# A fused wavelet, attention and expert-choice kernel: the second half of the token selection moved among the first expert chunks, rows split by columns, GpSimd's subtractions in pieces

## The chip, the core and the metric

One core of a Trainium2 chip runs one program. The metric is device time in microseconds (us), the median of 3 runs. Engines: TensorE (PE, matmuls; its weight loads are PEld), VectorE (DVE), ScalarE (ACT), GpSimd (POOL) and SyncE (SP, which only issues DMAs here). "Row L1535" means line 1535 of the kernel before.

## The reference, cut to what matters

```python
h = wavelet(x, ...)                                   # [32, 256, 256]
h = concat([cls_tok, h], axis=1)                      # [32, 257, 256]: 8224 rows
h = h + attention(layernorm(h), R)
h = h + moe(layernorm(h), ...)

def moe(x, gate_w, gamma, beta, fc1s, b1s, fc2s, b2s):
    scores = (tanh(x @ gate_w.T) + 1) * 0.5           # [8224, 8]
    vals, idx = top_k(scores.T, 1028)                 # each expert takes its 1028 best rows
    y = layernorm(x[idx], gamma, beta)
    h = gelu(y @ fc1[e].T + b1[e])                    # 256 -> 1024
    o = (h @ fc2[e].T + b2[e]) * vals                 # 1024 -> 256
    return x.at[idx].add(o)
```

## The kernel before

**Ahead of the change.** Wavelet and attention run image by image until some 295 us. The unfinished sum goes to `out`, normalised rows with their gates go to `rows` in HBM. `V` holds the gates as [128, 2, 257]: partition = expert within a half (4) x image (32), middle axis = the half `eh` (experts 0 to 3, experts 4 to 7). Twelve rounds of counting find each expert's threshold `Tf`.

**Selection (L1487 to L1526).** VectorE marks gates above and equal to the threshold (`ge`, `eq`), with their counts. TensorE sums the counts over an expert's images with the 0/1 matrices `same` and `before`. VectorE ranks the equal ones by a scan, keeps as many as are needed, adds them to `ge` and scans again. `TB` then holds, for each half, the exclusive rank of each token within its image, the image's number and the image's first slot in bf16, high and low part. `begM` and `finM` hold the first and last slot of an image, masked to one expert in each column. All of it is done for both halves at once, and then comes the first expert. `link` is a wait of VectorE for its own last instruction.

**Placing.** `one_hot` writes `oh` [128, 1028]: slot s belongs to image p. It takes two instructions, `ohu` (L1535) and `oh` (L1538). `place` treats one tile of 128 of the 1028 slots (eight tiles and one of 4): TensorE multiplies `oh` with `TB` into a PSUM bank (L1001), VectorE copies three columns out (`SM`, L1553), takes `rk` (L1556), counts the ranks not above it (`jk`, `pos`, L1560), computes the row's base (`rowf`, L1562) and adds them to the index (`idx`, L1566). Each tile of TensorE waits (`smc`) until VectorE has read the one before.

**Experts.** A `Job` is an expert (`q` = 0 to 7 in order of time) and a chunk `c` of it: 3 tiles (384 rows), 3 tiles (384), 3 tiles (260), `j` = 3q + c. An expert's weights sit in one of two buffer sets, by `eh`. Experts go in the order 0, 4, 1, 5, ... (`e = el + 4 * eh`), so each buffer set belongs to one half of `V`. All float matmuls are three products of high and low parts in fp32r. In `emit` every engine has the same frame: eight slices `f` for the current job, with work of the previous and next one laced in. TensorE: the first layer of slice f (`first`, six matmuls of 384 columns, L1022), a share of the previous job's second layer (`second`, L1036 for tokens, L1048 for the tail chunk), at f = 3 the turn (transposes, L1011) of the next job's rows, tiles to place, at f = 6 `tail_back` (L1059). ScalarE: `hidden` (gelu L756, copy `hh` L759), at f = 1 and 3 of jobs with c = 0 and c = 2 the copy `high` (L722) of one half of the next weights into fp32r, at f = 4 `high_rows` (L729), and `weighed` (L772). VectorE: `low_hidden` (the remainder `hl`, L1590), `with_bias`, `tail_bias` (L1612), `scaled` (gamma and beta on the turned rows, L1575) at f = 3, `low_rows` (L1583) at f = 5, and `place`. GpSimd, in its own order: scatters (L577), gathers (L555), and `low` (L536), which subtracts the copied high part from `raw`. `first` of slice f waits for `low_hidden` of slice f - 3.

**Weights.** `raw` [128, 2048] is one buffer in two halves. SyncE loads a half (L436) when GpSimd's `low` of that half is done (`wlo0`, `wlo1`), in the order w1, w2 of each expert. w2 of the next expert is split in the jobs with c = 2, w1 of the one after it in those with c = 0.

**Tiles to place.** The tiles of an expert are placed ahead of it, spread over the slices of a job by `spread`; when the last is placed, the next expert's one-hot follows. In the first expert's jobs, expert 1's nine tiles and expert 2's nine are placed in jobs 0, 1 and 2 (7, 5 and 6 of them), job 3 has none; from job 4 on there are 4 and 5 in the jobs with c = 1 and c = 2.

```python
both = [(3, t) for t in range(9)] + [(6, t) for t in range(9)]
tiles = both[(0, 7, 12)[k]:(7, 12, 18)[k]]
...
if split and u:
    low(1 - cur.eh, cur.q + 1, cur.c // 2, u - 1)
```

## Time and profile before

| | us |
|---|---|
| median of 3 runs | 784.48 (784.38 to 785.78) |
| the profiled execution | 786.62 |
| its span, first to last instruction | 784.8 |
| busy: TensorE / VectorE / ScalarE / GpSimd | 696.7 / 541.0 / 459.9 / 473.3 |
| mean granted TensorE clock | 0.944 |
| scatter L577, mean of 72 | 1.58 |
| GpSimd's L499, mean of 37 | 0.24 |
| GpSimd's subtraction L536 of w2, mean of 16 | 2.41 |

A row of a timeline gives the start and the length in us, the engine, the line, the operation, what it writes and reads with partitions x elements, and in brackets how long the engine had stood before it and what released it. "x6" are six instructions merged into one row. Instructions of an engine overlap a little: the next may start before the last one's record ends.

### The profile page before, as it was taken

Reading aid. Unit: us, or ns where it says so; the run is one execution under the profiler, and the core shown is the slowest. Engines: PE = TensorE matmul, PEld = TensorE weight load, DVE = VectorE, ACT = ScalarE, POOL = GpSimd, SP = SyncE. Lnnn points to the kernel's source line nnn. Section 1 sums busy time; section 2 is a strip of 40 time slices with the busy share of each in tenths; the row PEclk is TensorE's granted clock in tenths of the full one; section 3 lists DMA queues with packets and bytes.
Section 4 is the critical chain, followed back from the end, with each engine's and each line's share of the span. In section 5 each row is a group of like instructions: output and inputs, shape, how many; then the busy total and the mean of one; then the engine's idle time right before and its main releaser. Section 6 shows DMA issues by size and latency. Waiting matters only on the chain.

```text
span 784.8 us, 15827 instructions
## 1 busy us (share of the span) xinstructions
PE 696.7 (89%) x4630; PEld 635.5 (81%) x4630; DVE 541.0 (69%) x1885; ACT 459.9 (59%) x1095; POOL 473.3 (60%) x660
## 2 busy tenths in 40 slices
PE   6987999999999945447999999989999999999994
PEld 3986888888888734336989999989889999899993
DVE  3765798998899778987784766756846757634431
ACT  1003588888888869315556656665566566656551
POOL 0258689888988545142366485584674855846523
PEclk9989999999999975559999999999999999999997
DMA  9900022222222228121134243352342432533222
GB/s 258 307 18 1 4 83 81 80 80 81 80 80 81 81 93 170 54 56 61 30 81 117 42 109 89 50 149 43 75 122 41 108 88 42 146 52 49 35 28 27
DMA packets 63563, 64.14 MB, mean 82 GB/s; under 512 B 14032, under 2 KB 57104, under 8 KB 63376
## 3 DMA queue, kind: packets, MB, share of 16 engines
q1 hardware_dynamic: 50576, 46.33, 19.6%
q0 software_dynamic: 12800, 17.12, 13.5%
q8 instruction: 26, 0.43, 0.2%
q14 instruction: 33, 0.27, 0.1%
q10 hardware_dynamic: 128, 0.00, 0.0%
HBM read 37.90 MB, written 25.53 MB: 81 GB/s over the span
## 4 chain that ended last, share of the span: by engine, by line
PE 36%; DVE 7%; issue 6%; ACT 6%; POOL 5%; DMA 3%; POOLq 0%; ACTq 0%; DVEq 0%; SPq 0%
PE bank L1022 16%; PE bank L1036 15%; ACT bank L746 2%; PE bank L1011 2%; PE bank L1048 2%; POOL out L577 2%; POOL w2l L536 1%; POOL yg L555 1%; DMA raw<-in_fc1T 1%; DMA yg<-rows,idx 1%; DVE yl L1583 1%; ACT bank L756 1%; PE bank L1001 1%; DVE jk L1560 1%; ACT hh L759 1%
## 5 line engine op out<-in xcount | busy, mean ns | idle before, releaser
L577 POOL DMA_INDIRECT out<-ob,sidx x72 | 113.9, 1582 | 160.5 <-ACT ob L772 148.8
L1590 DVE TENSOR_TENSOR hl<-bank,hh 128x384 fp32r<-128x384 f32 (+1 forms) x192 | 97.5, 513 | 139.1 <-ACT hh L759 138.6
L756 ACT ACTIVATE bank<-bank,b1s 128x384 f32<-128x384 f32 (+1 forms) x192 | 99.4, 518 | 138.0 <-PE bank L1022 133.5
L1022 PE MATMUL bank<-yh,w1h 128*128 128x384 f32 (+1 forms) x384 | 132.7, 346 | 8.1 <-DVE hl L1590 4.7
L1022 PE MATMUL bank<-yh,w1l 128*128 128x384 f32 (+1 forms) x384 | 123.8, 322 | 0.0
L1022 PE MATMUL bank<-yl,w1h 128*128 128x384 f32 (+1 forms) x384 | 123.3, 321 | 0.0
L1036 PE MATMUL bank<-w2h,hh 128*128 128x256 f32 x384 | 108.1, 281 | 0.0
L1036 PE MATMUL bank<-w2l,hh 128*128 128x256 f32 x384 | 108.0, 281 | 0.0
L1036 PE MATMUL bank<-w2h,hl 128*128 128x256 f32 x384 | 107.9, 281 | 0.0
L555 POOL DMA_INDIRECT yg<-rows,idx x72 | 72.4, 1006 | 44.2 <-issue 39.1
L759 ACT ACTIVATE hh<-bank 128x384 fp32r<-128x384 f32 (+1 forms) x192 | 87.7, 457 | 6.1
L1022 PEld LDWEIGHTS bank<-yh,w1h 128*128 128x128 f32 x384 | 73.8, 192 | 13.0 <-DVE hl L1590 6.0
L1022 PEld LDWEIGHTS bank<-yl,w1h 128*128 128x128 f32 x384 | 73.6, 192 | 0.0
L1022 PEld LDWEIGHTS bank<-yh,w1l 128*128 128x128 f32 x384 | 73.1, 190 | 0.0
L1036 PEld LDWEIGHTS bank<-w2h,hh 128*128 128x128 f32 x384 | 72.7, 189 | 0.0
L1036 PEld LDWEIGHTS bank<-w2l,hh 128*128 128x128 f32 x384 | 72.7, 189 | 0.0
L1036 PEld LDWEIGHTS bank<-w2h,hl 128*128 128x128 f32 x384 | 72.5, 189 | 0.0
L880 PE MATMUL bank<-ET,Rw 128*128 128x256 f32 x256 | 66.1, 380 | 1.7 <-ACT ET L663 1.7
L948 PE MATMUL bank<-GT,ET 128*128 128x137 f32 (+1 forms) x256 | 52.5, 340 | 0.7 <-ACT GT L690 0.7
L504 POOL TENSOR_TENSOR ST<-A,mhalf 128x6 f32<-128x6 f32 x37 | 50.0, 1352 | 3.1
L880 PEld LDWEIGHTS bank<-ET,Rw 128*128 128x128 f32 x256 | 43.8, 191 | 5.6 <-issue 2.1
L290 POOL TENSOR_TENSOR ARENA<-OB,C 128x512 f32<-128x512 f32 x32 | 40.8, 1275 | 12.2 <-ACT OB L637 12.2
(249 smaller groups left out, 1770.6 us busy)
## 6 DMA issues: line engine op xcount, KB each, us to landing
BIG<-in_x SPq DMA_DIRECT2D x4, 2048.0 KB, 16.3
out<-Bs SPq DMA_DIRECT2D x32, 256.0 KB, 2.2
rows<-Yp SPq DMA_DIRECT2D x32, 256.0 KB, 2.4
raw<-in_fc1T SPq DMA_DIRECT2D x16, 512.0 KB
raw<-in_fc2T SPq DMA_DIRECT2D x16, 512.0 KB
yg<-rows,idx POOLq DMA_INDIRECT x72, 2.8
out<-ob,sidx POOLq DMA_INDIRECT x72, 3.8
gwb<-in_gate_w SPq DMA_DIRECT2D x1, 1024.0 KB, 7.2
```

What stands on the lines that cost most here:

```text
L290: return ops.tensor_tensor(OP[m.p].rearrange("p g (r k) -> p g r k", k=CG), blocks.unsqueeze(2).to_broadcast(wide), cst("blocks").rearrang ...
L504: g.tensor_tensor(st[:, 8:14], A6[:, :], mhalf[:, :], ALU.pow).then_inc(s["pow"], 1)
L555: g.indirect_dma_start(out=yg[eh][0:m, t, :], out_offset=None, in_=rows, in_offset=tok(ap=idx[eh][0:m, t:t + 1], axis=0))\
L577: g.indirect_dma_start(out=out_rows, out_offset=tok(ap=sidx[job.eh][0:m, t:t + 1], axis=0), in_=ob[t % 3][0:m, :], in_offset=None, compute ...
L746: last = A.activation(sgn[2 * eh + j], V[:, eh, :], ACT.Sign, bias=tried[:, k:k + 1], scale=-1.0, accum_out=cna[eh][:, j:j + 1])
L756: A.activation(h[:, 0:cur.w], h[:, 0:cur.w], ACT.Gelu_apprx_tanh, bias=b1s[:, bass.ds(cur.e, 1), f]).then_inc(s["hact"], 1)
L759: A.activation(hT[cur.p][0][:, f, 0:cur.w], h[:, 0:cur.w], ACT.Copy).then_inc(s["hhi"], 1)
L880: last = T.matmul(Rb[:, e * D:(e + 1) * D], Rw[:, j, e * P:(e + 1) * P], ET[c.p][:, j, 1:NT], start=(j == 0), stop=(j == 1))
L948: T.matmul(Sb[:, c0:c0 + w], ET[c.p][:, j, 1 + h * P:1 + (h + 1) * P], GT[c.p][:, j, 0:w], start=(j == 0), stop=False)
L1022: last = T.matmul(Lb[ring(cur, f)][:, 0:cur.w], w1s[cur.eh][i][:, d, f * P:(f + 1) * P], yT[cur.p][k][:, d, 0:cur.w], start=(n == 0), stop ...
L1036: mm = T.matmul(bank[4 + t % 2][:, 0:D], hT[prev.p][i][:, f, at:at + P], w2s[prev.eh][k][:, f, :], start=(n == 0), stop=(n == 23))
L1590: v.tensor_tensor(hT[cur.p][1][:, f, 0:cur.w], Lb[ring(cur, f)][:, 0:cur.w], hT[cur.p][0][:, f, 0:cur.w], ALU.subtract).then_inc(s["hlo"], 1)
```

## The change

- **Experts in order.** `e = q`; an expert's half of `V`, `TB`, `begM` is `q // 4`, its column `q % 4`. Buffers still alternate with `q`.
- **Selection by halves.** The chain is cut into `above`, `ranked_at`, `asked_for`, `taken`, `ranked`, `slots`, `slots_of_images`. For half 0 they run in one go, as before. For half 1 they are laced into VectorE's jobs 2 to 5; TensorE's three small matmuls for it go to jobs 3 and 5 (`asked`, `begun`), into columns of bank 7 between two tiles, with waits `tk_read` and `tc` on the next tile. The image's first slot is read from PSUM without a link.
- **Placing.** `SM` is gone: `rk` and `rowf` read the PSUM bank directly, and `rowf` comes ahead of `jk`. In the first expert's six jobs the tiles are 4, 5, 4, 5, 4, 5.
- **Rows split by columns.** `turn`, `scaled`, `high_rows`, `low_rows` signal for each of the two halves of the 256 columns; `first` of slice 0 waits for each half ahead of its three matmuls. In the first expert `low_rows` stands behind tile 5 instead of tile 6.
- **GpSimd's `low`** is four instructions of 256 columns instead of one of 1024; only the last signals.
- **Tail's bias ahead.** `tail_bias` stands ahead of `low_hidden` of its slice instead of behind.
- `keep_index` of expert 1 waits for its nine indices.

```diff
+PIECE = 256
-                self.e = self.el + 4 * self.eh
+                self.e = self.q
+                self.half, self.group = (self.q // 4, self.q % 4) if isinstance(self.q, int) else (1, self.q - 4)
...
-                if isinstance(el, int) and el == 0 and k < 3:
-                    both = [(3, t) for t in range(9)] + [(6, t) for t in range(9)]
-                    tiles = both[(0, 7, 12)[k]:(7, 12, 18)[k]]
+                if isinstance(el, int) and el == 0:
+                    tiles = [(3 + k // 2 * 3, t) for t in ((0, 1, 2, 3), (4, 5, 6, 7, 8))[k % 2]]
...
-                rest = g.tensor_tensor(flat(lo, half), raw[:, half * NF:(half + 1) * NF], flat(hi, half), ALU.subtract)
+                for c0 in range(0, NF, PIECE):
+                    rest = g.tensor_tensor(flat(lo, half)[:, c0:c0 + PIECE], raw[:, half * NF + c0:half * NF + c0 + PIECE],
+                                           flat(hi, half)[:, c0:c0 + PIECE], ALU.subtract)
                 rest.then_inc(s[f"wlo{half}"], 1)
...
+                elif job.q == 1:
+                    po.wait_ge(s["ixd"], 2 * 9)
...
-                act.wait_ge(s["yr"], job.j + 1)
                 after(act, "hmm", (job.j - 1) * 8)
                 for d in range(2):
-                    last = A.activation(yT[job.p][0][:, d, 0:job.w], bank[2 + d][:, 0:job.w], ACT.Copy)
-                last.then_inc(s["yhi"], 1)
+                    act.wait_ge(s["yr"], job.j * 2 + d + 1)
+                    A.activation(yT[job.p][0][:, d, 0:job.w], bank[2 + d][:, 0:job.w], ACT.Copy).then_inc(s["yhi"], 1)
...
+            def asked(half, total):
+                pe.wait_ge(s["tk_c"], 2 * half + 1)
+                T.matmul(total[:, 0:1], cst("same"), cgt[:, half:half + 1], start=True, stop=True)
+                T.matmul(total[:, 1:2], cst("before"), tot[:, half:half + 1], start=True, stop=True).then_inc(s["tk_mm"], 1)
+            def begun(half, total):
+                pe.wait_ge(s["tk_c"], 2 * half + 2)
+                T.matmul(total[:, 2:3], cst("before"), tot[:, half:half + 1], start=True, stop=True).then_inc(s["tk_mm"], 1)
+            asked(0, bank[2])
+            begun(0, bank[2])
...
+                if t == 4 and isinstance(job.q, int) and job.q == 2:
+                    pe.wait_ge(s["tk_read"], 2)
+                if t == 4 and isinstance(job.q, int) and job.q == 3:
+                    pe.wait_ge(s["tc"], 2)
...
+                    if f == 0 and n % 3 == 0:
+                        pe.wait_ge(s["yt"], cur.j * 2 + d + 1)
...
-                    pe.wait_ge(s["yt"], cur.j + 1)
...
+                    if at_job(cur, 3) and f == 0:
+                        pe.wait_ge(s["smc"], 2 * 9 + 4)
+                        asked(1, bank[7])
+                    if at_job(cur, 5) and f == 0:
+                        pe.wait_ge(s["smc"], 3 * 9 + 4)
+                        begun(1, bank[7])
...
+            def slots_of_images(half, total):
+                h, n = slice(half, half + 1), slice(NT + 1, NT + 2)
+                dve.wait_ge(s["tk_c"], 2 * half + 2)
+                dve.wait_ge(s["tk_mm"], 2 * half + 2)
+                v.tensor_tensor(fin[:, h], total[:, 2:3], tot[:, h], ALU.add)
+                v.tensor_copy(beg[:, h], total[:, 2:3])
+                link(v.tensor_copy(TB[:, half, n], total[:, 2:3]))
+                link(v.tensor_copy(mm2[:, h], TB[:, half, n]))
+                v.tensor_tensor(TB[:, half, NT + 2:NT + 3], beg[:, h], mm2[:, h], ALU.subtract)
+                for e in range(2):
+                    last = v.tensor_tensor((begM, finM)[e][:, :, half], (beg, fin)[e][:, h].to_broadcast([P, 5]),
+                                           cst("owner"), ALU.mult)
+                last.then_inc(s["tc"], 1)
+                dve.wait_ge(s["tc"], half + 1)
...
-                v.tensor_copy(SM[0:m, t, :], B[0:m, NT:NT + 3]).then_inc(s["row"], 1)
-                dve.wait_ge(s["row"], r0 + 1)
-                v.tensor_scalar(rk[0:m, t:t + 1], cst("slot")[0:m, t:t + 1], SM[0:m, t, 1:2], SM[0:m, t, 2:3],
-                                ALU.subtract, ALU.subtract).then_inc(s["row"], 1)
-                dve.wait_ge(s["row"], r0 + 2)
+                v.tensor_scalar(rk[0:m, t:t + 1], cst("slot")[0:m, t:t + 1], B[0:m, NT + 1:NT + 2], B[0:m, NT + 2:NT + 3],
+                                ALU.subtract, ALU.subtract)
+                v.tensor_scalar(rowf[0:m, t:t + 1], B[0:m, NT:NT + 1], float(NT), -1.0, ALU.mult, ALU.add)\
+                    .then_inc(s["row"], 1)
+                dve.wait_ge(s["row"], n + 1)
                 v.tensor_scalar(jk[0:m, :], B[0:m, 0:NT], rk[0:m, t:t + 1], None, ALU.is_le, ALU.add,
                                 accum_out=pos[0:m, t:t + 1]).then_inc(s["smc"], 1)
-                v.tensor_scalar(rowf[0:m, t:t + 1], SM[0:m, t, 0:1], float(NT), -1.0, ALU.mult, ALU.add)\
-                    .then_inc(s["row"], 1)
...
                 for f in SLICES:
+                    if prev and prev.c == 2 and f in OT_AT[0:2]:
+                        tail_bias(prev, OT_AT.index(f))
                     if cur:
                         low_hidden(cur, f)
...
+                    if at_job(cur, 2) and f == 0:
+                        above(1)
+                    if at_job(cur, 2) and f == 2:
+                        ranked_at(1)
+                    if at_job(cur, 3) and f == 1:
+                        asked_for(1, bank[7])
+                    if at_job(cur, 3) and f == 3:
+                        taken(1)
+                    if at_job(cur, 4) and f == 2:
+                        ranked(1)
+                    if at_job(cur, 4) and f == 5:
+                        slots(1)
+                    if at_job(cur, 5) and f == 1:
+                        slots_of_images(1, bank[7])
```

## Rows read from the trace of the kernel before

**Rows 1.** Windows: time, busy us of each engine, granted clock, DMA share, GB/s.
```profile
348.50:367.50 19.00, 13.28 (x61) 10.89 (x62) 16.23 (x59) 9.76 (x18) 8.66 (x7) 0.86 0.24 77
366.20:370.80 4.60, 4.60 (x22) 4.17 (x21) 3.05 (x14) 1.94 (x4) 0.00 (x0) 0.63 0.00 0
367.50:387.50 20.00, 20.00 (x133) 19.20 (x133) 14.55 (x49) 9.71 (x20) 4.66 (x4) 0.94 0.09 14
421.80:440.40 18.60, 18.60 (x131) 18.10 (x132) 10.98 (x36) 10.04 (x22) 8.99 (x7) 1.00 0.33 65
456.40:474.15 17.75, 16.29 (x111) 15.19 (x109) 11.39 (x21) 11.45 (x23) 15.94 (x10) 1.00 0.48 135
```

**Rows 2.** Line L722, ScalarE's copies of weights: what ended its idle time before them.
```profile
  DMA raw<-in_fc1T: 24.1, 12
```

**Rows 3.** Timeline of GpSimd at the boundary from expert 1 to 2.
```profile
457.06 2.43 POOL L536 TENSOR_TENSOR w2l<-raw,w2h 128x1024 fp32r<-128x1024 f32 x1
459.65 1.84 POOL L577 DMA_INDIRECT out<-ob,sidx  x1 [0.17 <-issue]
...
462.83 2.42 POOL L536 TENSOR_TENSOR w2l<-raw,w2h 128x1024 fp32r<-128x1024 f32 x1
```

**Rows 4.** Timeline of ScalarE at the same boundary.
```profile
468.73 1.06 ACT L722 ACTIVATE w1h<-raw 128x1024 fp32r<-128x1024 f32 x1 [2.14 <-DMA raw<-in_fc1T]
```

**Rows 5.** Timeline of VectorE: two one-hots, and the boundary.
```profile
350.84 0.73 DVE L1535 TENSOR_SCALAR ohu<-iot,begM 128x1028 bf16<-128x1028 f32 x1
...
457.51 2.54 DVE L1535 TENSOR_SCALAR ohu<-iot,begM 128x1028 bf16<-128x1028 f32 x1
460.09 1.29 DVE L1538 SCALAR_TENSOR_TENSOR oh<-iot,finM,ohu 128x1028 bf16<-128x1028 f32 x1
...
472.53 0.56 DVE L1590 TENSOR_TENSOR hl<-bank,hh 128x384 fp32r<-128x384 f32 x1 [0.78 <-ACT hh L759]
```

**Rows 6.** Timeline of TensorE: first expert, chunk 3's start, and the boundary.
```profile
343.31 1.54 PE L1011 MATMUL bank<-C,yg 128*128 128x128 f32 x6 [1.07 <-DMA yg<-rows,idx]
...
348.52 0.66 PE L1022 MATMUL bank<-yh,w1h 128*128 128x384 f32 x1 [1.03 <-DVE yl L1583]
...
365.67 0.28 PE L1001 MATMUL bank<-TB,oh 128*128 128x260 bf16 x1 [1.90 <-DVE jk L1560]
...
404.26 0.34 PE L1022 MATMUL bank<-yh,w1h 128*128 128x384 f32 x1
...
461.77 0.44 PE L1022 MATMUL bank<-yh,w1h 128*128 128x384 f32 x1 [0.74 <-DVE hl L1590]
...
474.15 0.44 PE L1022 MATMUL bank<-yh,w1h 128*128 128x384 f32 x1 [0.42 <-DVE yl L1583]
```

**Rows 7.** Timeline of VectorE in the selection.
```profile
324.98 0.48 DVE L1491 TENSOR_SCALAR_CACHE_REDUCE ge<-V,Tf 128x257 f32<-128x257 f32 x1
...
328.33 0.88 DVE L1504 SCALAR_TENSOR_TENSOR eq<-sc,need,eq 128x257 f32<-128x257 f32 x2
...
329.98 1.28 DVE L1509 TENSOR_TENSOR_SCAN sc<-one,ge 128x257 f32<-128x257 f32 x2
...
333.30 0.42 DVE L1535 TENSOR_SCALAR ohu<-iot,begM 128x384 bf16<-128x384 f32 x1
```

**Rows 8.** Timeline of VectorE: the first instruction of two tiles in a row.
```profile
336.23 0.15 DVE L1553 COPY SM<-bank 128x3 f32<-128x3 f32 x1
...
337.53 0.15 DVE L1553 COPY SM<-bank 128x3 f32<-128x3 f32 x1
```

**Rows 9.** Timelines of VectorE and GpSimd where both work, in the attention.
```profile
59.98 1.25 DVE L1172 TENSOR_SCALAR cyp<-ch,cst,cpw 128x256 f32<-128x256 f32 x1
61.05 0.65 POOL L478 TENSOR_TENSOR ARENA<-BIG 128x256 f32<-128x256 f32 x1
...
284.24 0.62 DVE L1262 TENSOR_TENSOR GM<-dm,sg 128x448 f32<-128x448 f32 x1
284.27 0.68 POOL L499 TENSOR_SCALAR A<-ST 128x4 f32<-128x4 f32 x1 [3.23 <-ACT Bs L645]
```

More of the change, by code:

```diff
@@ L324, in place_bank, with at_job @@
             return bank[6 + t % 2] if isinstance(job.q, int) and job.q == 0 else bank[7]
+        def at_job(job, j):
+            return job and isinstance(job.j, int) and job.j == j
         SLICES = range(NF // P)
@@ L1012, in turn @@
                                            ident[0:m, 0:m])
[L1013 removed]
+                    last.then_inc(s["yt_t"], 1)
             def first(cur, f):
@@ L1496, in _ @@
-            dve.wait_ge(s["tk_c"], 1)
-            for eh in range(2):
-                last = v.tensor_tensor_scan(sc[:, eh, :], one[:, :], eq[:, eh, :], 0.0, ALU.mult, ALU.add)
-            dve.wait_ge(s["tk_mm"], 1)
-            v.tensor_scalar(need[:, :], bank[2][:, 0:2], -1.0, float(KTOK), ALU.mult, ALU.add)
-            link(v.tensor_copy(mm2[:, :], bank[3][:, 0:2]))
-            link(v.tensor_tensor(need[:, :], need[:, :], mm2[:, :], ALU.subtract))
-            for eh in range(2):
-                last = v.scalar_tensor_tensor(out=eq[:, eh, :], in0=sc[:, eh, :], scalar=need[:, eh:eh + 1],
-                                              in1=eq[:, eh, :], op0=ALU.is_le, op1=ALU.mult)
@@ new lines, in ranked_at, with asked_for @@
+            def ranked_at(half):
+                dve.wait_ge(s["tk_c"], 2 * half + 1)
+                link(v.tensor_tensor_scan(sc[:, half, :], one[:, :], eq[:, half, :], 0.0, ALU.mult, ALU.add))
+            def asked_for(half, total):
+                h = slice(half, half + 1)
+                dve.wait_ge(s["tk_mm"], 2 * half + 1)
+                v.tensor_scalar(need[:, h], total[:, 0:1], -1.0, float(KTOK), ALU.mult, ALU.add)
+                v.tensor_copy(mm2[:, h], total[:, 1:2]).then_inc(s["tk_read"], 1)
+                dve.wait_ge(s["tk_read"], half + 1)
+                link(v.tensor_tensor(need[:, h], need[:, h], mm2[:, h], ALU.subtract))
@@ new lines, in taken, with ranked @@
+            def taken(half):
+                h = slice(half, half + 1)
+                link(v.scalar_tensor_tensor(out=eq[:, half, :], in0=sc[:, half, :], scalar=need[:, h],
+                                            in1=eq[:, half, :], op0=ALU.is_le, op1=ALU.mult))
+                link(v.tensor_tensor(ge[:, half, :], ge[:, half, :], eq[:, half, :], ALU.add))
+            def ranked(half):
+                link(v.tensor_tensor_scan(sc[:, half, :], one[:, :], ge[:, half, :], 0.0, ALU.mult, ALU.add))
+                v.tensor_copy(tot[:, half:half + 1], sc[:, half, NT - 1:NT]).then_inc(s["tk_c"], 1)
@@ L1529, in _ @@
+            above(0)
+            ranked_at(0)
+            asked_for(0, bank[2])
+            taken(0)
+            ranked(0)
+            slots(0)
+            slots_of_images(0, bank[2])
             s["ohu"] = sem("slots_begun")
```

80 lines of the change are left out of this document (23 added, 57 removed).

## The prediction

> **What bounds the kernel now.** First the table by stage. TensorE is busy in 18.60 of 18.60 us in a middle chunk (from 421.8), but in 16.29 of 17.75 us in the first chunk of an expert (from 456.4); the very first chunk (348.5 to 367.5) has 13.28 of 19.00 us at a granted clock of 0.86, and there VectorE is busy for 16.23 us [rows 1]. So time can be won in the selection and the first chunk, where VectorE leads, and in the first chunk of each expert, where TensorE stalls. What leads there, the waits of ScalarE say: its copies of the first layer's weights waited 24.1 us, 12 times, for their DMA [rows 2]. Followed back at one boundary: GpSimd's second subtraction of w2 ends at 462.83 + 2.42 = 465.25 [rows 3]; the DMA into the freed half of `raw` follows; ScalarE has it at 468.73, after a wait of 2.14 us [rows 4]; on that hang VectorE's remainder of slice 5 at 472.53 [rows 5] and the next chunk's first matmul at 474.15, 0.42 us late [rows 6]. VectorE's stretched one-hot (2.54 us; 0.73 us where GpSimd lets it be [rows 5]) costs TensorE 0.74 us at 461.77 [rows 6], ahead of that wait. The rest stands on this reading: a stall of TensorE before the wait is slack, a delay of GpSimd is not.
>
> **Selection by halves.** On the path lie 324.98 to 333.30 [rows 7]. Out of it go two counting reductions (0.4 from start to start each, 0.8; estimate from the row of 0.48), the wait for the other half's threshold (0.2, estimate), one of two mask products (0.88 to 0.44), half of the addition that follows (0.3, estimated by the product's price for the same columns), one of two scans (1.28 to 0.64) [rows 7], and links at the end, 0.2. The twin of the other scan ran beside TensorE's totals: nothing. Sum -2.6; bounds -1.8 and -3.2.
>
> **Placing a tile.** It takes 1.30 us, 336.23 to 337.53 [rows 8]. The copy goes, and `rowf` moves off the end; I take -0.22 (estimate: the copy's 0.15 and its link). Pointer operands out of PSUM are in no row: between -0.3 and +0.1. The first gathers follow GpSimd's own pace, so only one tile counts at the start: -0.2.
>
> **Rows split by columns.** Today the turn begins at 343.31 and the first matmul comes 5.2 us later [rows 6]. By columns, scaling starts after half a turn (0.77 of 1.54) and the matmuls after half of the remainders. But TensorE must first place tile 8, which waits for VectorE's tile 6, and that now stands behind `low_rows`. Counted through (turn 1.54, scaling 0.6, ScalarE and VectorE 0.5 each, 0.9 of a tile, the placement) it is 4.4: -0.8. At later first chunks the matmuls need only the first `low_rows`, half of the two: -0.47 each.
>
> **First experts' tiles evenly.** The first chunk loses three of seven tiles, 3 x 1.30 = 3.9 us of VectorE, and the four left are 0.9 cheaper: -4.7, since VectorE set the pace (at 365.67 TensorE had waited 1.90 us for a tile [rows 6]). ScalarE, the next in line, is busy for 9.76 us there [rows 1], so it takes none of it back. Chunk 1 ran 20.0 us at clock 0.94, where the same shape takes 18.60 at 1.00 [rows 1]: without the stalls before it, -1.3 (nothing, if the clock falls all the same). Chunk 2 (367.5 + 20.0 to 404.26, 16.7 us) held six tiles and gets four, like the later ones that take 16.0 [rows 1, 6]: -0.7.
> What moves in: chunk 3, the first of expert 1, had no tile and gets five, with the other half's totals and masks, and a one-hot. Behind ScalarE's late weights there is no room. After a remainder like that of 472.53 [rows 5] come its own 0.5, `low_rows` 1.0, 0.9 of a tile until TensorE may place the last one, the placement 0.1 and the last slice 1.05: 476.1 instead of 474.15. With GpSimd's 0.2 there, +2.1. TensorE's wait for `tk_read` vanishes in that. Chunk 5: TensorE's first placement waits for `slots_of_images`, eight small operations (some 0.95) behind `low_hidden`; the second layer covers part: +1.0. Chunk 4's scan and subtraction (1.2 us) fall where TensorE leads: nothing; without that cover they would cost themselves. No DMA changes its place in a queue; `keep_index` now waits for nine tiles, as the scatters behind it do anyway.
>
> **GpSimd's subtractions in pieces.** This decides. One of 1024 columns takes 2.43 us [rows 3], one of 256 (other strides) 0.65 [rows 9]; four cost between -0.1 and +0.4 more than one, I take +0.15. The point is who waits. Today the one-hot, issued 0.45 us into the subtraction, stands until its end [rows 3, 5]. In pieces it gets in: at 59.98 a VectorE operation waited for a GpSimd one and was through 0.18 us after the next of GpSimd's had begun at 61.05 [rows 9]. Then both one-hot operations run inside the subtraction, and GpSimd stands: at 284.27 a GpSimd operation whose mean is 0.24 lasted 0.68 us, until 0.09 after the end of VectorE's product of two SBUF tensors that had started at 284.24 [rows 9]. `oh`, from `iot` and `ohu`, is of that kind (1.29 us [rows 5]); `ohu` once let in holds 0.56. So GpSimd's chain grows by 0.56 + 1.15 + 2 x 0.15, less 0.26 by which today's `oh` stretches the scatter of 459.65 (1.84 us [rows 3], mean 1.58): 1.75 us. It passes through DMA and ScalarE to TensorE, less the 0.47 above: +1.28 at each of the five boundaries with a one-hot, +6.4. Bounds: 5 x -0.47 = -2.4, if nothing is put back, and 5 x 1.9 = +9.5, if pieces and both operations count whole.
> The Trainium skill, "SBUF — State Buffer", section "Who interferes with whom", speaks against this edit: a VectorE instruction with two SBUF inputs contends with a GpSimd one that reads SBUF, and the one that comes first blocks the other for its whole length. By that rule, with 0.73 + 1.29 us of blocking, the sum below would be 1.5 us higher; the trace agrees in direction [rows 9].
>
> **Tail's bias ahead.** It lets `tail_back` go earlier, but in time that lies before the wait for ScalarE: nothing at the boundaries. At the last boundary, which has no weights to wait for, -0.3 with the rows by columns.
>
> **Sum.** -2.6 - 0.2 - 0.8 - 4.7 - 1.3 - 0.7 + 2.1 + 1.0 = -7.2; +6.4 - 0.3 gives -1.1 us. The profiled span of 784.8 goes to 783.7 (that execution took 786.62, 1.8 around the span, and is 2.1 above the median); the median of 784.48 goes to **783.4**. A measurement of this kernel tells 0.2%, 1.6 us, from no change: the forecast is two large terms that nearly cancel.
>
> **Rivals.** *VectorE waits out all four pieces.* GpSimd's next piece could claim the port before VectorE does. Then the chain grows by 0.3 only, each boundary gives -0.2, and the sum is -7.2 - 1.0 - 0.3: 776.0. For it: the next piece stands ready in GpSimd's queue; against it: [rows 9]. *Slower: TensorE's clock.* After the stalls ahead of 365.67 the granted clock fell towards the lower of its two levels (1.2 GHz; 0.63 over 366.2 to 370.8), and chunk 1 took 1.4 longer [rows 1, 6]. With the chain 1.75 us later TensorE stands nearly as long at a boundary. If the clock falls at all five, +1.3 each: 789.9. It decides once those stalls reach the first chunk's; today's boundary keeps 1.00 [rows 1]. *The first chunk doesn't shorten*, as ScalarE's weight copies and TensorE's placements in order hold it: +4.7 + 1.3, 789.4.
>
> **Chances.** Forecast case 0.45, its own range 779.5 to 787 (early part -9 to -5, boundaries +4 to +8.5): 0.19 faster, 0.17 same, 0.09 slower. Pieces waited out: 0.25, faster. Clock: 0.20, slower. First chunk: 0.10, of it 0.03 same and 0.07 slower. Together 0.44, 0.20 and 0.36. The range 775.5 to 790.5 takes in the three prices and leaves out the ends beyond.
>
> **What would show it.** Selection 5.7 us from the first `is_gt` to `ohu`; first matmul 3.6 us earlier; chunk 1 begins 8.3 earlier; chunk 3 takes 2 us longer, with TensorE's waits for `jk`. `ohu` stays under 1.4 us everywhere, the four pieces around it spread over 4 us or more, and ScalarE waits 3.5 to 4 us for the second half of `raw` instead of 2.14. If that wait stays where it is, the boundary term is wrong; if chunk 1 begins under 6 us earlier, the first.

## The result: slower by 0.7%, and the profile after

| | before | after |
|---|---|---|
| median of 5 runs, us | 785.78 (784.38 to 786.82) | 791.48 (790.54 to 793.04) |
| ratio | | 1.0072 (95% interval 1.0055 to 1.0088) |
| span of the profiled execution | 784.8 | 789.7 |
| TensorE / VectorE / GpSimd busy | 696.7 / 541.0 / 473.3 | 697.9 / 526.0 / 492.7 |

The forecast was 783.4, 1.1 us less than the 784.48 of before; measured in the same comparison, the kernel is 5.7 us slower, and its time ended 1.0 us above the top of the range. VectorE has 15 us less work, GpSimd 19 us more.

The page of the kernel after, its costliest groups (instructions x count, then busy us and mean ns, then idle time before them):

```profile
L542 POOL TENSOR_TENSOR w2l<-raw,w2h 128x256 fp32r<-128x256 f32 x64 | 52.3, 849 | 0.5
```

The waits ahead of line L731, ScalarE's weight copies, which answer to [rows 2] (24.1 us, 12 times):

```profile
  DMA raw<-in_fc1T: 39.4, 12
```

The boundary from expert 1 to 2, which answers to [rows 3 to 6]. First GpSimd's timeline:

```profile
452.72 4.37 POOL L542 TENSOR_TENSOR w2l<-raw,w2h 128x256 fp32r<-128x256 f32 x4
457.25 1.58 POOL L586 DMA_INDIRECT out<-ob,sidx  x1 [0.16 <-issue]
459.13 1.00 POOL L562 DMA_INDIRECT yg<-rows,idx  x1 [0.30 <-issue]
460.16 2.78 POOL L542 TENSOR_TENSOR w2l<-raw,w2h 128x256 fp32r<-128x256 f32 x4
```

Then VectorE's:

```profile
452.69 0.73 DVE L1584 TENSOR_SCALAR ohu<-iot,begM 128x1028 bf16<-128x1028 f32 x1
453.46 1.65 DVE L1587 SCALAR_TENSOR_TENSOR oh<-iot,finM,ohu 128x1028 bf16<-128x1028 f32 x1
...
464.01 0.56 DVE L1631 TENSOR_TENSOR hl<-bank,hh 128x384 fp32r<-128x384 f32 x1 [5.14 <-ACT hh L767]
...
506.86 1.25 DVE L1584 TENSOR_SCALAR ohu<-iot,begM 128x1028 bf16<-128x1028 f32 x1
508.24 1.55 DVE L1587 SCALAR_TENSOR_TENSOR oh<-iot,finM,ohu 128x1028 bf16<-128x1028 f32 x1
```

The last two are of the next boundary (chunk 9), where GpSimd's four pieces are:

```profile
506.79 4.29 POOL L542 TENSOR_TENSOR w2l<-raw,w2h 128x256 fp32r<-128x256 f32 x4
```

Then ScalarE's:

```profile
461.95 1.06 ACT L731 ACTIVATE w1h<-raw 128x1024 fp32r<-128x1024 f32 x1 [5.28 <-DMA raw<-in_fc1T]
466.46 1.06 ACT L731 ACTIVATE w1h<-raw 128x1024 fp32r<-128x1024 f32 x1 [1.51 <-DMA raw<-in_fc1T]
```

And TensorE's first matmul of this chunk and of the next:

```profile
451.92 0.34 PE L1044 MATMUL bank<-yh,w1h 128*128 128x384 f32 x1
...
471.33 0.44 PE L1044 MATMUL bank<-yh,w1h 128*128 128x384 f32 x1
```

The one-hot gets in, as forecast. At this boundary `ohu` starts 0.03 us ahead of the pieces and takes 0.73 us; at the other four it starts 0.07 to 0.09 us behind the first piece and takes 1.24 or 1.25, so it waits for one piece and gets in before the next. Before, it took 2.51 to 2.54 at all five. GpSimd pays: four pieces without company take 2.78 us, those beside the one-hot 4.28 to 4.37, so 1.5 to 1.6 more.

How this reaches TensorE, in us from the first matmul of the chunk (means of the five boundaries, read from the timelines as above):

| | before | after | difference |
|---|---|---|---|
| GpSimd's second subtraction of w2 ends | 8.88 | 10.98 | +2.10 |
| ScalarE's second weight copy starts | 12.52 | 14.64 | +2.12 |
| from there to the next chunk's first matmul | 5.40 | 4.89 | -0.51 |
| the whole chunk | 17.91 | 19.53 | +1.61 |

ScalarE's waits for `raw` show it in another place than the prediction looked. The one for the *first* half grew, from 1.58 us to 5.28 here and from a mean of 1.80 to 4.12 over the five; the one for the second fell from 2.14 to 1.51 here, but has a mean of 2.55 against 2.23. In front of the first copy ScalarE's later slices queue (VectorE stands 5.14 us for `hh`).

Chunk by chunk, from the first matmul of a job to the first of the next in TensorE's timeline (the sums in the rest of the text are of these lengths; the last four columns are the experiments a, b, k and n below):

```
chunk      before  after  | one_piece  pieces_alone  one_hot_between  order_on_before
0           19.00  14.79  |  15.83      19.24         14.01            19.01
1           20.04  19.05  |  18.99      19.75         19.05            19.05
2           16.70  15.38  |  15.37      16.70         15.37            16.70
3           17.54  22.38  |  21.48      19.43         19.49            15.63
5           15.98  17.16  |  17.15      15.99         17.17            15.98
6           17.78  19.41  |  17.27      19.68         15.63            15.79
9           18.26  19.68  |  17.92      20.28         16.66            16.28
12          18.27  19.46  |  18.54      20.12         16.05            16.25
13          18.55  19.93  |  18.61      18.57         18.61            18.55
15          17.61  19.70  |  17.92      19.69         16.53            15.79
18          17.66  19.40  |  17.48      19.72         15.48            15.62
21          16.31  16.59  |  16.15      16.69         15.49            15.64
```

The first matmul comes 3.80 us earlier (344.72), chunks 0 to 2 win 6.52 more; chunk 3 gives back 4.84, chunk 5 1.18, the five boundaries (6, 9, 12, 15, 18) 8.07, chunk 13 1.38, chunk 21 0.28. Windows of TensorE's clock, in the columns of [rows 1], for the kernel after: chunk 0, the start of chunk 1, chunk 3, chunk 6, chunk 13, and three stretches of 3.4 us in the last three.

```profile
344.72:359.51 14.79, 12.69 (x59) 11.56 (x59) 11.56 (x37) 9.85 (x19) 9.36 (x13) 0.80 0.27 87
358.20:362.80 4.60, 4.46 (x29) 4.17 (x29) 3.93 (x11) 3.22 (x7) 0.00 (x0) 1.00 0.36 134
393.93:416.32 22.39, 18.61 (x119) 17.15 (x118) 15.22 (x50) 12.08 (x24) 18.33 (x23) 0.92 0.47 129
451.92:471.33 19.41, 17.41 (x110) 16.80 (x108) 9.34 (x20) 10.81 (x22) 18.18 (x21) 0.91 0.45 123
579.82:599.75 19.93, 19.93 (x130) 19.43 (x131) 10.93 (x33) 10.77 (x23) 9.63 (x8) 0.93 0.29 60
...
412.10:415.50 3.40, 3.40 (x14) 2.56 (x13) 3.10 (x12) 1.78 (x5) 1.42 (x3) 0.50 0.32 105
463.30:466.70 3.40, 3.40 (x15) 3.40 (x14) 2.28 (x4) 1.82 (x5) 3.07 (x4) 0.50 0.70 230
579.40:582.80 3.40, 2.98 (x11) 2.98 (x12) 1.85 (x4) 2.93 (x7) 2.73 (x3) 0.50 0.40 135
```

Around the start of chunk 1 the clock is 1.00, where the like stretch of the kernel before had 0.63. But it falls to the lower level in three places where it had not before: in chunk 3 (behind a stand of TensorE of 3.02 us, shown further down), in chunk 6 (behind one of 1.86) and at the start of chunk 13 (within one of 0.88, which ends at 579.82). In chunk 13, where TensorE is busy throughout, this is the 1.38 us. In chunk 6 it costs nothing that can be seen: from the second weights to the next chunk it takes 4.88 us, as in chunks 9, 12 and 15 (4.87), which keep 0.99 or 1.00. For chunk 3 see below.

### The profile page after: what moved, and what is told of

It is laid out like the page before. It is cut to its first block, busy times and chain, and to the rows that moved or that the text cites. A ratio compares the mean times of both kernels' runs of the same rounds, so it can differ in the third digit from the quotient of the medians.

```text
span 789.7 us, 15779 instructions
## 1 busy us (share of the span) xinstructions
PE 697.9 (88%) x4636; PEld 638.2 (81%) x4636; DVE 526.0 (67%) x1827; ACT 459.8 (58%) x1095; POOL 492.7 (62%) x756
## 3 DMA queue, kind: packets, MB, share of 16 engines
q0 software_dynamic: 12800, 17.12, 13.1%
## 4 chain that ended last, share of the span: by engine, by line
PE 34%; POOL 8%; issue 7%; DVE 6%; ACT 4%; DMA 3%; POOLq 1%; ACTq 0%; SPq 0%; DVEq 0%
PE bank L1044 15%; PE bank L1058 14%; POOL out L586 3%; POOL w2l L542 3%; POOL yg L562 2%; DMA raw<-in_fc1T 2%; PE bank L1031 2%; DMA yg<-rows,idx 2%; ACT bank L764 1%; DVE ge L1461 1%; PE bank L1070 1%; PE bank L1021 1%; ACT hh L767 1%; DVE T L1478 1%; DVE yl L1625 1%
## 5 line engine op out<-in xcount | busy, mean ns | idle before, releaser
L562 POOL DMA_INDIRECT yg<-rows,idx x72 | 71.7, 996 | 40.3 <-DVE idx L1609 21.2
L1044 PEld LDWEIGHTS bank<-yh,w1h 128*128 128x128 f32 x384 | 74.6, 194 | 13.1 <-DVE hl L1631 7.3
L542 POOL TENSOR_TENSOR w2l<-raw,w2h 128x256 fp32r<-128x256 f32 x64 | 52.3, 849 | 0.5
```

What stands on the lines that cost most here:

```text
L542: rest = g.tensor_tensor(flat(lo, half)[:, c0:c0 + PIECE], raw[:, half * NF + c0:half * NF + c0 + PIECE], flat(hi, half)[:, c0:c0 + PIECE] ...
L562: g.indirect_dma_start(out=yg[eh][0:m, t, :], out_offset=None, in_=rows, in_offset=tok(ap=idx[eh][0:m, t:t + 1], axis=0))\
L1044: last = T.matmul(Lb[ring(cur, f)][:, 0:cur.w], w1s[cur.eh][i][:, d, f * P:(f + 1) * P], yT[cur.p][k][:, d, 0:cur.w], start=(n == 0), stop ...
```

## The experiments

**What the pieces cost.** Three kernels: the changed one with one subtraction per half; the kernel before with the four pieces alone; the changed one with two pieces.

```diff
-PIECE = 256
+PIECE = 1024     # a_one_piece; 512 in c_two_pieces
```

> The changed kernel with GpSimd's subtraction whole again (one instruction of 1024 columns). Theory (GpSimd, let wait by the one-hot between its pieces, leads the first chunk of each expert through raw's DMA and ScalarE's copy): the first subtraction of w2 falls from 4.37 to 2.43 us, ohu is 2.4 to 2.5 us again at five places, and the first chunks of experts 2 to 6 lose 8.1 + 1.4 us against the changed kernel and some 2.4 more through the rows split by columns, chunk 3 about 0.8: 10 to 13 us off, about 779 to 781. Rival (the pieces are harmless, the added time comes from the tiles in chunk 3 and a fallen clock): within 2 us of the changed kernel, 789 to 792.

Measured: 781.41 us, ratio to before 0.9945 (0.9932 to 0.9959). That is 0.4 above the expected range. The rest of the change is a gain of 0.55%; the pieces cost 1.27%, 10 us.

> The kernel before with nothing but the subtraction in four pieces of 256 columns. Theory: first subtraction of w2 about 4.4 us at six boundaries (405 included, where the one-hot also falls in it), 1.9 + 2 x 0.37 - 0.26 = 2.4 us later at the second DMA, with no 0.47 from the split rows to set against it: 6 x 2.4, less the 0.4 to 1.3 us of slack that TensorE's stalls ahead of it hold, about +12 us, 796 to 799, more if the clock falls. Rival (VectorE's stretched one-hot led the boundary): 0.6 to 0.9 us off at each of six, 780 to 782.

Measured: 797.36 us, ratio 1.0146 (1.0131 to 1.0162): each of the five first chunks with a one-hot is 1.85 to 2.1 us longer. The pieces harm by themselves.

> The changed kernel with two pieces of 512 columns. Theory: ohu is let in after the first half, oh after the second, when the subtraction is done: the first subtraction of w2 is stretched by ohu alone, 2.4 + 0.12 + 0.55 = 3.1 us, the second 2.5; then the scatter waits behind oh for some 0.3 to 0.8. About half of what the four pieces cost comes back: 784 to 787. Rival (each further instruction costs, the one-hot doesn't): two thirds of a smaller loss come back, subtraction 2.55 us both times.

Measured: 781.67 us, ratio 0.9944 (0.9928 to 0.9959). A miss: I took two pieces for half of the harm, and they do none. The one-hot doesn't get in between them. VectorE's timeline in that kernel:

```profile
452.46 3.14 DVE L1584 TENSOR_SCALAR ohu<-iot,begM 128x1028 bf16<-128x1028 f32 x1
```

And GpSimd's:

```profile
452.50 2.54 POOL L542 TENSOR_TENSOR w2l<-raw,w2h 128x512 fp32r<-128x512 f32 x2
```

So it is the one-hot's entry that costs, and not a second instruction. Here too, and with one piece, `ohu` starts 0.04 us ahead of the subtraction (in a_one_piece it takes 3.03), so which record starts first doesn't tell who stands.

**Whole, but behind the one-hot.** One piece; at the five boundaries GpSimd waits for the one-hot (`ohd`) before the first half of w2. This is the order that the pieces bring about, without pieces.

```diff
+                    if split and u == 1 and cur.c == 2 and (not isinstance(cur.q, int) or cur.q == 1):
+                        po.wait_ge(s["ohd"], cur.q + 4)
```

> The subtraction whole (1024 columns), but the first one of w2 at the five boundaries waits until the one-hot of that chunk is written, so VectorE goes first and GpSimd stands, as the four pieces bring it about. Theory: ohu 0.73, oh 1.29 there, the subtraction 2.4 long but starting 2.0 us later; the boundaries cost what they cost in the changed kernel less 0.37 x 2 for the pieces: 787 to 790, far above the kernel with one piece. Rival (it is the number of instructions): same time as with one piece.

Measured: 790.72 us, ratio 1.0073 (1.0056 to 1.0091), the ratio of the changed kernel, and 0.7 us above the expected range. ScalarE's waits for `raw` are 38.3 us, nearly those of the changed kernel (39.4), with `ohu` at 0.74 to 0.76. The five chunks have a mean of 19.51 us against 19.53. GpSimd's timeline:

```profile
453.19 2.40 POOL L542 TENSOR_TENSOR w2l<-raw,w2h 128x1024 fp32r<-128x1024 f32 x1 [2.12 <-DVE oh L1589]
```

**Chunk 3.** Two kernels with one piece: in the first, expert 1's and 2's tiles go 5, 6, 7, 0 over chunks 0 to 3; in the second `taken(1)`, the mask product and addition, moves from chunk 3 to chunk 4.

```diff
-                    tiles = [(3 + k // 2 * 3, t) for t in ((0, 1, 2, 3), (4, 5, 6, 7, 8))[k % 2]]
+                    both = [(3, t) for t in range(9)] + [(6, t) for t in range(9)]
+                    tiles = both[(0, 5, 11)[k]:(5, 11, 18)[k]]
...
```
```diff
-                    if at_job(cur, 3) and f == 3:
+                    if at_job(cur, 4) and f == 1:
                         taken(1)
```

> One piece, and the first experts' eighteen tiles in jobs 0 to 2 (5, 6 and 7 of them) with none in job 3; the other half's selection stays where the change puts it. Theory (in chunk 3 TensorE's placements wait behind VectorE, which ScalarE's late weights hold up): chunk 3 falls from 21.5 to 18 to 18.5 us, chunks 0 to 2 grow by 1 to 2 together; 779 to 780 against 781.4 with one piece. Rival (the other half's selection is what holds chunk 3): chunk 3 keeps over 20 us and the kernel gets slower, 783.

Measured: 781.13 us, ratio 0.9937 (0.9923 to 0.9950). Chunk 3 fell to 17.00 as expected, but chunks 0 to 2 took 16.55, 20.47 and 17.01: the four sum to 71.0, against 71.7 in a_one_piece. The tiles cost where they go what they saved, and the forecast of 779 to 780 is missed. Chunk 3 still holds the other half's totals and masks here, and takes less than the 17.54 of before.

> One piece, tiles as the change has them, but the mask product and addition of the other half (taken) stand in job 4 instead of job 3. Theory (tiles, not selection): chunk 3 loses at most their 0.9 us, 21.5 to 20.6 or more, 780.5 to 781.5 in all. Rival (selection holds it, by two-tensor operations that wait for GpSimd's w1 subtraction): chunk 3 back to 18.5, 778.

Measured: 780.17 us, ratio 0.9921 (0.9906 to 0.9936); chunk 3 takes 20.66 instead of 21.48, chunk 4 is unchanged. The gain over a_one_piece (0.9945) isn't clear of noise, and the shorter chunk isn't owed to the edit: d_whole_but_behind_one_hot, which has `taken` in chunk 3 and is a_one_piece up to chunk 5, takes 20.60 there. What differs is the clock. Chunk 3 in a_one_piece, d and f:

```profile
396.09:417.57 21.48, 18.57 (x120) 17.34 (x119) 14.56 (x48) 12.06 (x24) 15.99 (x10) 0.92 0.51 142
394.08:414.68 20.60, 17.20 (x119) 16.10 (x118) 14.35 (x48) 11.95 (x24) 16.17 (x11) 1.00 0.53 145
395.04:415.71 20.67, 17.18 (x119) 16.08 (x118) 13.00 (x46) 11.96 (x24) 16.36 (x11) 1.00 0.53 145
```

**The second half ahead (two misses).** If GpSimd's chain sets the end, an earlier second half should gain. Both halves of w2 one behind the other, ahead of the third scatter and gather; once with a_one_piece, once with e_tiles_in_three_jobs.

```diff
+                    if split and cur.c == 2 and u == 1:
+                        for half in range(2):
+                            low(1 - cur.eh, cur.q + 1, 1, half)
...
```

> One piece; in the jobs with c = 2 GpSimd subtracts both halves of w2 one after the other, ahead of the third scatter and gather. Theory (GpSimd's chain to raw leads the first chunk): the second DMA starts 2.9 to 3.3 us earlier, ScalarE's wait for it goes from 2.1 to 0, and each first chunk of experts 1 to 6 loses its stalls, 0.5 to 1.5 us: 774 to 778 against 781.4. Rival (TensorE or VectorE leads there anyway): within 1 us of 781.4; if the third scatter now leads, slower.

> Both edits together: tiles in three jobs, second half of w2 ahead of the third scatter. Theory: the gains add up but for chunk 3, which both shorten: 772 to 777. Rival: no better than the better of the two.

Measured: g 797.01 us, ratio 1.0153 (1.0129 to 1.0176), and h 799.15 us, ratio 1.0172 (1.0149 to 1.0194). ScalarE's wait for the second half is gone, but VectorE's one-hot stands for both subtractions, and TensorE waits for the remainder behind it. In g_second_half_ahead, GpSimd's timeline:

```profile
451.15 4.73 POOL L542 TENSOR_TENSOR w2l<-raw,w2h 128x1024 fp32r<-128x1024 f32 x2
```

VectorE's at the same place:

```profile
451.09 5.36 DVE L1587 TENSOR_SCALAR ohu<-iot,begM 128x1028 bf16<-128x1028 f32 x1
```

TensorE's there, and in chunk 21, where there is no one-hot:

```profile
458.16 0.44 PE L1047 MATMUL bank<-yh,w1h 128*128 128x384 f32 x1 [3.17 <-DVE hl L1634]
...
735.87 1.16 PE L1034 MATMUL bank<-C,yg 128*128 128x128 f32 x6 [2.82 <-DMA yg<-rows,idx]
```

The last row is a second fault of that order: the third gather comes so late that the turn of the next rows waits for it. Two later kernels take both away, one at a time.

**The order of GpSimd.** With f_masks_in_chunk_4, in the jobs with c = 2: in j only the third scatter goes behind the second half; in k the first half goes ahead of the second scatter too.

```diff
                 for u in range(3):
-                    if prev and not tail:
+                    last = split and cur.c == 2
+                    if last and u == 1:                      # k alone
+                        low(1 - cur.eh, cur.q + 1, 1, 0)
+                    if prev and not tail and not (last and u == 2):
                         scatter(prev, prev.t0 + u)
                     if far:
                         gather(far, far.t0 + u)
-                    if split and u:
+                    if split and u and not (last and u == 1):  # j: as before
                         low(1 - cur.eh, cur.q + 1, cur.c // 2, u - 1)
+                    if prev and not tail and last and u == 2:
+                        scatter(prev, prev.t0 + u)
```

> f_masks_in_chunk_4 (780.2) with one order changed on GpSimd: in the jobs with c = 2 the third scatter goes behind the second half of the w2 subtraction, so the third gather and that subtraction come some 1.9 us earlier. The run g_second_half_ahead lost 16 us where 4 to 7 were to be won; two things had happened there together: the one-hot was shut out for 5.36 us by two subtractions back to back, and the third gather came 5 us later, so that the turn of the next rows waited 2.8 us for it (also in chunk 21, which has no one-hot). Theory: GpSimd's second subtraction, through the DMA into raw and ScalarE's copy, sets the end of a first chunk; with the gather early and no two subtractions back to back it gives what was expected: first chunks 0.6 to 1.0 us shorter, 775.5 to 777.5. Rival: the stretched one-hot (3.04 us) and not that chain sets it: first chunks unchanged, 779.5 to 781.

> As j_third_scatter_last, and the first half of the w2 subtraction also goes ahead of the second scatter, where GpSimd had stood for 0.7 us, so that the one-hot falls on a scatter and a gather instead of on a subtraction. Theory: ohu takes under 1 us instead of 3.04, TensorE's wait for hl (0.88 us) goes, ScalarE's waits for raw (2.0 and 2.1 us) shrink to under 1: first chunks 1.0 to 1.5 us shorter than in f_masks_in_chunk_4, 773 to 776. Rival: the second gather, now 2 us later, or the second scatter's buffer holds something up: no better than j_third_scatter_last, 777 or more.

Measured: j 791.15 us, ratio 1.0063 (1.0050 to 1.0076); k **769.42** us, ratio 0.9796 (0.9777 to 0.9814). k gained more than the theory said (773 to 776). j missed both forecasts: chunk 6 fell to 16.60 and chunk 21 to 15.49, as the theory had it, but chunks 9 to 18 rose to 21.1 to 22.3. There GpSimd got ahead of `oh` and kept it out. VectorE's timeline of j, at chunk 9:

```profile
502.01 2.89 DVE L1587 TENSOR_SCALAR ohu<-iot,begM 128x1028 bf16<-128x1028 f32 x1
505.03 4.20 DVE L1590 SCALAR_TENSOR_TENSOR oh<-iot,finM,ohu 128x1028 bf16<-128x1028 f32 x1
```

GpSimd's, there:

```profile
504.50 1.27 POOL L562 DMA_INDIRECT yg<-rows,idx  x1 [0.16 <-issue]
505.79 2.35 POOL L542 TENSOR_TENSOR w2l<-raw,w2h 128x1024 fp32r<-128x1024 f32 x1
508.31 2.42 POOL L586 DMA_INDIRECT out<-ob,sidx  x1 [0.17 <-issue]
```

Between the end of `ohu` (504.90) and `oh` lie 0.13 us, where chunk 6 has 0.03 (450.80 + 3.03 to 453.86) and `oh` took 1.29. That this gap let GpSimd in is my reading; no run changed it alone. In k, with the one-hot beside a scatter and a gather, `ohu` takes 0.73 us at its quickest and 0.93 at its slowest, `oh` 1.29 everywhere. What is stretched at these boundaries now is the scatter and the gather, to 1.95 and 1.92 us at most, where 1.58 and 1.00 are usual. VectorE's timeline of k, at chunk 6:

```profile
449.20 0.73 DVE L1589 TENSOR_SCALAR ohu<-iot,begM 128x1028 bf16<-128x1028 f32 x1
449.97 1.29 DVE L1592 SCALAR_TENSOR_TENSOR oh<-iot,finM,ohu 128x1028 bf16<-128x1028 f32 x1
```

ScalarE's, there:

```profile
453.06 1.06 ACT L736 ACTIVATE w1h<-raw 128x1024 fp32r<-128x1024 f32 x1
459.20 1.06 ACT L736 ACTIVATE w1h<-raw 128x1024 fp32r<-128x1024 f32 x1 [1.53 <-DMA raw<-in_fc1T]
```

The first half of the weights is there before ScalarE asks for it. All of ScalarE's waits for `raw` together are 8.4 us in k. Chunk 21, which has no one-hot, is 0.7 us shorter than in a_one_piece in j and in k alike, so there the third scatter's new place gives it all; in chunk 6 that place gives 0.7 and the first half's another 1.0. The first half's new place alone was not run.

**The order with pieces, on the kernel before, and with other tiles.** m is k with `PIECE = 256`; n is the kernel before with k's order on GpSimd and nothing else; l is f_masks_in_chunk_4, and o is k, with expert 2's tiles 7 and 2 over chunks 2 and 3 (and TensorE's waits moved with them).

> k_one_hot_between (769.4) with GpSimd's subtractions in four pieces of 256 columns again, as in the changed kernel. Theory: what the pieces cost (10 us between the changed kernel and a_one_piece) is mostly the one-hot, let in between them, that holds GpSimd back; here the one-hot stands beside a scatter and a gather, so the pieces cost no more than their own length, 0.37 us a subtraction, and half of that is slack: 769 to 771.5. Rival: the pieces cost by themselves or through the remainders of VectorE that mix with them: 774 or more.

Measured: 769.95 us, ratio 0.9789 (0.9766 to 0.9812). Away from the one-hot the pieces cost nothing that can be told. The group of w2's pieces has a mean of 736 ns instead of 849:

```profile
L542 POOL TENSOR_TENSOR w2l<-raw,w2h 128x256 fp32r<-128x256 f32 x64 | 45.0, 736 | 0.5
```

> The kernel before with GpSimd's new order alone: the first half of the w2 subtraction ahead of the second scatter, the third scatter behind the second half. Theory: what the boundaries lose to GpSimd's chain and to the stretched one-hot is in the kernel before as well, and the order takes it out there too: first chunks 6 to 18 and 21 shorter by 1 to 1.6 us each, 776 to 779. Rival: it needs the rows split by columns to pay, since without them the first matmul of the next chunk waits for low_rows: 781 to 784.

Measured: 773.16 us, ratio 0.9832 (0.9810 to 0.9854), better than expected: 13 us (11.5 to 14.9) from the order of GpSimd's instructions alone. Chunk 3 gains 1.91 us too. In its profile chunk 1 is 0.99 us shorter as well, at a clock of 1.00 instead of 0.95, but that lies ahead of the first instruction that the edit moves, so it is not its work.

> f_masks_in_chunk_4 with expert 2's tiles 7 and 2 instead of 4 and 5 over chunks 2 and 3 (the other half's totals stay in chunk 3). Theory: chunk 2 has room for three tiles more at a cost of 0.3 to 1.3 us (before it held six tiles in 16.7 us, now four in 15.37), and chunk 3 loses three tiles that stood behind ScalarE's late weights, 2.0 to 3.0 us of its 20.66: 778 to 779.5. Rival: what leaves chunk 3 comes back whole in chunk 2, as in e_tiles_in_three_jobs, where four chunks together stayed the same: 780 to 781.

> k_one_hot_between with expert 2's tiles 7 and 2 over chunks 2 and 3. In l_seven_tiles_in_chunk_2 chunk 3 fell to 16.86 us, but chunk 2 took 1.6 and chunk 4 1.6 more (chunk 4 by a lower clock). In k_one_hot_between chunk 3 still has 19.49. Theory: chunk 3 falls by 2 to 3 us, chunk 2 rises by 1.6, and chunk 4 keeps 18.44, as TensorE no longer stands before it: 768 to 769. Rival: the clock falls in chunk 4 all the same: 769.5 to 770.5.

Measured: l 779.83 us, ratio 0.9919 (0.9900 to 0.9938); o 769.36 us, ratio 0.9785 (0.9759 to 0.9810), each between its theory and its rival. No gain over the kernels they start from. Chunk 3 falls to 16.86 and 16.56, but chunk 2 rises to 17.01 in both and chunk 4 to 20.03 and 19.39. My expectation of o put the latter down to the clock, wrongly: it is 1.00 there. TensorE stands for VectorE, whose remainder now comes behind tiles, one-hot and masks. TensorE's timeline of l in chunk 4:

```profile
417.19 0.44 PE L1045 MATMUL bank<-yh,w1h 128*128 128x384 f32 x1 [1.20 <-DVE hl L1632]
```

**Rows split by columns, undone**, with one piece: `turn`, `scaled`, `high_rows`, `low_rows` signal once per job, and in the first expert `low_rows` stands behind tile 6 again.

```diff
-                    if f == 0 and n % 3 == 0:
-                        pe.wait_ge(s["yt"], cur.j * 2 + d + 1)
...
+                    pe.wait_ge(s["yt"], cur.j + 1)
```

> The changed kernel with whole subtractions of 1024 columns (as in a_one_piece, 781.4), and with the rows no longer split by columns: turn, scaled, high_rows and low_rows signal once per job again, the first matmuls wait for both halves, and in the first expert low_rows stands behind tile 6. The prediction gave this part -0.8 us at the first chunk and -0.47 at each of five later first chunks: then this run is 3.1 us above a_one_piece, 784.5. Rival, from a_one_piece's first chunks (together only 0.45 us shorter than before, of which the split should be all): the matmuls of slice 0 are not what the end hangs on, and the part is worth 0 to 0.5 us at the boundaries and 0.8 at the start: 782.3.

Measured: 784.12 us, ratio 0.9971 (0.9958 to 0.9983), against 0.9945 for a_one_piece: the split is worth 0.26%, 2.0 us, between the two expectations. (The profiled spans, 781.7 and 780.6, show 1.1 of it.) The traces show what it does at a boundary: from ScalarE's second weight copy to the next chunk's first matmul it takes 5.41 us in chunks 6 to 15 with the rows whole, before and here, and 4.87 with them split, in a_one_piece and in the kernel after. One exception: chunk 12 of a_one_piece takes 6.06, and ScalarE had waited 0.17 us for that copy, so something else sets the end there; what, no run shows.

## Why the prediction was wrong, point by point

The early part came out as forecast. Two terms failed by their size. Chunk 3 was put at +2.1 us and took 4.84, because the sum had only the tiles in it, and not the later weights or the clock. The delay of GpSimd's chain at each of the five boundaries was put at 1.75 us and was 2.10. And the fall of TensorE's clock, kept out of the sum as a rival, cost 1.38 us in chunk 13. Term by term:

- **Selection by halves**: forecast -2.6, found -1.96 (324.30 to 330.66, 6.36 us against 8.32), within its bounds. The 0.2 for the other half's threshold is saved too, but ahead of the first of these rows. The 0.2 of links at the end is not: VectorE stands for TensorE's total and behind it there. VectorE's timeline of the kernel after:

```profile
326.42 0.16 DVE L1532 TENSOR_SCALAR need<-bank 128x1 f32<-128x1 f32 x1 [0.51 <-PE bank L997]
...
329.48 0.16 DVE L1559 TENSOR_TENSOR fin<-bank,tot 128x1 f32<-128x1 f32 x1 [0.35 <-PE bank L1002]
329.87 0.16 DVE L1560 COPY beg<-bank 128x1 f32<-128x1 f32 x1 [0.23 <-issue]
```

  The first of these waits the prediction had right: it gave the other scan of the equal ones "nothing", since it ran beside TensorE's totals, and from scan to `need` it takes 1.21 us where it took 1.19.
- **First matmul** 3.6 earlier: 3.80, of which 0.68 lies ahead of the selection's first row; in a_one_piece the selection begins 1.21 us later than here (325.51) and the first matmul comes 2.63 earlier than before. **Placing**: 1.04 us a tile for 1.30, right. **First chunk** -4.7: -4.21; **chunk 1** -1.3: -0.99; **chunk 2** -0.7: -1.32; **chunk 5** +1.0: +1.18. The early part's mechanisms held, but that its sum of 10.3 is met to 0.1 us is partly luck: between the runs with four tiles in it chunk 0 varies with the clock, from 14.0 us at 0.90 (k, d) over 14.8 at 0.80 (the kernel after) to 15.8 at 0.73 (a_one_piece), and the early part of a_one_piece wins 8.2.
- **Chunk 3** +2.1: +4.84. This is the largest miss, 2.7 us. The reading, that tiles behind ScalarE's late weights have no room, was right; two effects were left out. ScalarE's timeline of the kernel before, at its second weights in that chunk:

```profile
416.46 1.06 ACT L722 ACTIVATE w1h<-raw 128x1024 fp32r<-128x1024 f32 x1 [2.22 <-DMA raw<-in_fc1T]
```

ScalarE's of the kernel after, and of d_whole_but_behind_one_hot (one piece, clock 1.00):

```profile
408.07 1.06 ACT L731 ACTIVATE w1h<-raw 128x1024 fp32r<-128x1024 f32 x1 [3.04 <-DMA raw<-in_fc1T]
...
407.21 1.06 ACT L733 ACTIVATE w1h<-raw 128x1024 fp32r<-128x1024 f32 x1 [2.14 <-DMA raw<-in_fc1T]
```

TensorE's of the kernel after:

```profile
411.52 0.28 PE L1021 MATMUL bank<-TB,oh 128*128 128x260 bf16 x1 [3.02 <-DVE jk L1606]
```

  The second weights come 14.1 us after the chunk's start, where they came 12.2 after it (416.46 against 404.26): 1.9 us more. In d, with one piece, it is 13.1, so 0.9 of it comes without the pieces (the chunk before had become 1.3 shorter, while GpSimd's chain had not) and 1.0 with them; the prediction charged the pieces only to the five boundaries with a one-hot. From the second weights to the next chunk it took 5.3 us before, 7.5 in d and 8.2 after: 2.1 for the tiles, as forecast, and 0.8 for the clock, which falls in this chunk here and not in d. Together 4.8. `taken` costs nothing that can be told: f_masks_in_chunk_4, without it, has the same 7.5.
- **GpSimd's pieces** +1.28 at each of five boundaries, +6.4: found +8.07, 1.61 each, and 10 us for the pieces in all. "The one-hot gets in, and GpSimd stands" is what happened (d_whole_but_behind_one_hot costs as much, m_one_hot_between_in_pieces costs nothing). What failed is the size of GpSimd's delay, 1.75 forecast and 2.10 found. Its terms: pieces 0.37 longer than one (2.78 against 2.41), not 0.15; the two one-hot instructions hold GpSimd for 1.51 to 1.59 us, where the prediction had 0.56 + 1.15 = 1.71; the scatter's relief 0.26, right; and the first subtraction starts 0.12 later in the chunk than before (in a_one_piece and i_rows_whole too), which was left out. That makes 1.51 + 2 x 0.37 - 0.26 + 0.12 = 2.11. The rows' -0.47 was right: -0.51, and 2.12 - 0.51 is the 1.61 that was found.
- **The path** was the forecast one, GpSimd's second subtraction, DMA, ScalarE's copy, TensorE: 2.10 us later at its start and 2.12 at the copy. The sign that it named was wrong: it had ScalarE's wait for the second half at 3.5 to 4 us, where the mean is 2.55, since the copy before it had moved as well. That the wait of 1.51 at this boundary is short has a cause of its own: the transfer into the freed first half was issued at 457.25 and was there at 461.95, 4.7 us later, where in a_one_piece it took 3.3 (456.54 to 459.83). The scatter and the gather went out beside it in both; why it was slower there no run shows.
- **The rule of the Trainium skill** ("SBUF — State Buffer", "Who interferes with whom") spoke against this edit, and with its 1.5 us more the forecast would have been 784.9, nearer to what was found. Its direction is shown; the 1.51 to 1.59 us of blocking are less than the 2.02 it would give.
- **Rivals**: that VectorE waits out all four pieces is refuted, though it does wait out two of 512 columns. The clock rival came true in part: of the five boundaries the clock fell in chunk 6, at no cost that can be seen, and behind chunk 12 (chunk 13, +1.38), and besides them in chunk 3 (0.8). The first chunk did shorten.
- **Tail's bias ahead** -0.3: from the first matmul of job 23 to the end of the span it is 32.6 us in both. Chunk 21, the last boundary, is 0.16 us shorter in a_one_piece; with the pieces, which the prediction gave no price there, it is 0.28 longer.
- **Whole**: without the pieces the forecast comes to -9.9 (-7.2, 5 x -0.47 and -0.3); a_one_piece has -0.55%, 4.3 us. What is missing in its profile is the early part (2.1), chunk 3 (1.8) and the boundaries (1.9). At these the rows give their 0.4 to 0.5 in four of five, but GpSimd's chain starts 0.1 later, chunk 12 has its exception, and the transfer before the second copy takes 0.7 us longer than before in chunk 15.

## What to carry to other kernels

Where a VectorE instruction and a GpSimd subtraction fell together here, splitting the one in four only changed who stood, and splitting it in two changed nothing; put such a pair where neither is on the path. The order of three instructions in GpSimd's queue, with not one of them changed, was worth 13 us (1.7%), against 0.55% for all of the change without its pieces. By the traces the first half of a weight freed early starts the transfer early, and the one-hot falls on a scatter and a gather; the two were not taken apart on the kernel before. Before an edit that lets a waiting engine in, ask what the engine that then stands is releasing. And before a shorter chunk is put down to an edit, compare its granted clock: in chunk 3 a fall of 3.4 us passed for the price of two instructions.
